# A second gather without a bound: an extra table row for edges whose source has no row of its own

## The reference

```python
x = _layernorm(x + _L0_gnn_ref(x, ...))          # mean of messages per node
# two relational attention layers, and a residual norm
h = x
for l in range(2):
    xw = einsum('nf,rfg->rng', h, W[l])
    out_j = xw[edge_type, src]; out_i = xw[edge_type, dst]
    logits = leaky_relu(out_i @ q[l] + out_j @ k[l])
    alpha = segment_softmax(logits, dst)
    h = relu(segment_sum(alpha * out_j, dst) + b[l])
x = _layernorm(x + h)
```

## Time and profile before

| | |
|---|---|
| median of 3 runs | 981.58 us (974.68 to 982.33) |
| the profiled execution | 986.6 us, span 984.5 us |
| TensorE's granted clock, mean | 0.835 of full speed |
| VectorE busy | 808.0 us (82%) |
| TensorE busy | 692.9 us (70%) |
| ScalarE busy | 613.8 us (62%) |
| GpSimd busy | 588.7 us (60%) |
| gathers of layer 0, first to last start | 325.4 to 481.5 us |
| gathers of layer 1, first to last start | 636.9 to 797.8 us |

### The profile page before, as it was taken

One profiled execution on the slowest core, in us unless ns is written; L12 is line 12 of the kernel. 1 busy time (PEld: TensorE's weight loads), 2 busy tenths in 40 slices (PEclk: granted clock), 3 DMA queues, 4 the chain that ended last, 5 costly groups with the idle time before them and its releaser, 6 DMA issues.

```text
span 984.5 us, 11352 instructions
## 1 busy us (share of the span) xinstructions
PE 692.9 (70%) x3092; PEld 444.9 (45%) x3092; DVE 808.0 (82%) x2191; ACT 613.8 (62%) x1396; POOL 588.7 (60%) x506
## 2 busy tenths in 40 slices
PE   3546657655664598898888889658899797678830
PEld 2425545444443365564554456434555453334410
DVE  4589997988889787889799999686878879999960
ACT  1569988997798755565557587554556463434440
POOL 4767777777770688888400000088887834876674
PEclk9657876787685599999999999769999897989975
DMA  8266666656554323225344554432222420143210
GB/s 222 83 207 192 200 194 203 200 171 198 174 158 133 99 79 99 84 69 183 114 133 125 162 163 135 140 103 87 68 67 96 157 69 28 48 136 90 64 39 28
DMA packets 87742, 123.00 MB, mean 125 GB/s; under 512 B 14174, under 2 KB 66826, under 8 KB 87679
## 3 DMA queue, kind: packets, MB, share of 16 engines
q1 hardware_dynamic: 69455, 99.35, 32.3%
q0 software_dynamic: 15680, 21.55, 7.8%
q10 hardware_dynamic: 2544, 1.38, 0.6%
HBM read 87.79 MB, written 45.04 MB: 135 GB/s over the span
## 4 chain that ended last, share of the span: by engine, by line
DVE 29%; POOL 23%; issue 18%; PE 10%; ACT 9%; DMA 8%; SPq 1%; POOLq 0%; DVEq 0%; ACTq 0%
POOL xs L461 19%; DVE ys L1121 5%; DVE work L1295 5%; POOL xd L461 4%; PE ps_y L714 4%; ACT stage L795 4%; DMA xs<-h_table,posI 3%; DVE st L1102 3%; DVE ys L1268 2%; DVE opT L1295 2%; DVE st L1071 2%; DMA xs<-x_table,posI 2%; ACT xd L811 2%; DVE st L1061 2%; DVE stage L1065 1%
## 5 line engine op out<-in xcount | busy, mean ns | idle before, releaser
L795 ACT ACTIVATE stage<-stage,nm,rs 128x128 f32<-128x128 f32 x800 | 320.8, 486 | 21.8 <-DVE nm L1056 21.8
L714 PE MATMUL ps_y<-work,wr 128*128 128x512 f32 (+1 forms) x528 | 232.7, 573 | 31.2 <-DVE work L1295 31.1
L461 POOL DMA_INDIRECT xs<-h_table,posI x98 | 132.7, 1354 | 183.9 <-DMA h_table<-ys 154.4
L461 POOL DMA_INDIRECT xs<-x_table,posI x98 | 127.6, 1302 | 62.2 <-DMA x_table<-xd 32.6
L1295 DVE SCALAR_TENSOR_TENSOR work<-typB,xs 128x896 f32<-128x896 uint8 x132 | 142.9, 1087 | 26.3 <-PE ps_y L714 18.9
L714 PEld LDWEIGHTS ps_y<-work,wr 128*128 128x128 f32 x528 | 100.7, 202 | 131.4 <-issue 73.5
L530 POOL DMA_INDIRECT out<-xd,outI x98 | 113.7, 1160 | 61.5 <-issue 28.7
L714 PE MATMUL ps_y<-opT,wr 128*128 128x512 f32 (+1 forms) x256 | 118.4, 588 | 23.7 <-DVE opT L1295 23.7
L461 POOL DMA_INDIRECT xs<-in_x,srcI x98 | 105.6, 1077 | 47.4 <-issue 28.4
L461 POOL DMA_INDIRECT xd<-in_x,dstG x98 | 107.3, 1095 | 29.9 <-issue 29.0
L1061 DVE BATCH_NORM_STATS2 st<-stage 128x6 f32<-128x128 f32 x400 | 82.9, 278 | 19.5 <-DMA stage<-in_x 19.1
(11 more groups left out here) (206 smaller groups left out, 1132.7 us busy)
## 6 DMA issues: line engine op xcount, KB each, us to landing
stage<-in_x SPq DMA_DIRECT2D x39, 640.0 KB, 4.1
out<-stage SPq DMA_DIRECT2D x39, 640.0 KB, 3.0
xs<-alpha_rows SPq DMA_DIRECT2D x28, 448.0 KB, 4.9
x_table<-xd SPq DMA_DIRECT2D x14, 448.0 KB, 3.0
h_table<-ys SPq DMA_DIRECT2D x14, 448.0 KB, 3.7
work<-in_src SPq DMA_DIRECT2D x13, 448.0 KB
ys<-in_edge_attr SPq DMA_DIRECT2D x6, 896.0 KB, 9.0
sameB<-same_rows SPq DMA_DIRECT2D x42, 112.0 KB
```

The lines of the kernel that those rows point to most:

```text
L461: nc.gpsimd.indirect_dma_start(out=buf[:, t, :], out_offset=None, in_=table, in_offset=bass.IndirectOffsetOnAxis(ap=idx[:, t:t + 1], axis= ...
L714: mm = pe.matmul(ps_y[:, u, lo:hi], wr[:, r, :], rows, start=(r == 0), stop=(r == R - 1))
L795: ins = a.activation(slot(c)[:, r, :], slot(c)[:, r, :], ACT.Identity, bias=nm[:, h, n:n + 1], scale=rs[:, h, n:n + 1])
```

## The change

`h1_table` gets row EP, and SP stores one partition of `relu_row` there once, late in stage A. VectorE makes a second list of indices for the second gather, min(pos, EP), in `dstG`, which stage A no longer needs. The layer-1 gather reads by `dstG` without a bound, so every row of `xs` is written. ScalarE's 14 fills, the semaphore `refill` and the order REFILLS are gone. The layer-0 gather is as it was.

```diff
-    REFILLS = [g for g in range(NG) if g != SPARE] + [SPARE]
...
-    h1_table = nc.dram_tensor("h1_table", (EP, D), F32).ap()
+    h1_table = nc.dram_tensor("h1_table", (EP + 1, D), F32).ap()
...
-        h1_rows = h1_table.rearrange("(t p) d -> p t d", p=P)
+        h1_rows = h1_table[0:EP].rearrange("(t p) d -> p t d", p=P)
...
                 if g == NG - 1:
+                    sp.dma_start(h1_table[EP:EP + 1, :], relu_row[0:1, 0, :]).then_inc(bare_out, 16)
                     sp.wait_ge(p_ready, 1)
                     sp.dma_start(wr[:], w_rel[0].rearrange("r f g -> f r g")).then_inc(w0_in, 16)
...
             for j in range(2):
-                pool.wait_ge(p_ready, 1)
+                pool.wait_ge(p_ready, j + 1)
                 for u in range(2):
                     pool.wait_ge(tab_out[j][u], 16 * NG // 2)
                 for g in range(NG):
-                    pool.wait_ge((a_norm, refill)[j], g + 1 if j == 0 else REFILLS.index(g) + 1)
-                    gather(g, xs, (x1_table, h1_table)[j], posI, xs_in[j + 1], EP - 1)
+                    if j == 0:
+                        pool.wait_ge(a_norm, g + 1)
+                        gather(g, xs, x1_table, posI, xs_in[1], EP - 1)
+                    else:
+                        if g == 0:
+                            pool.wait_ge(bare_out, 16)
+                        gather(g, xs, h1_table, dstG, xs_in[2])
...
-                def fill(g):
-                    copy(grp(xs, g), mid(relu_row[:, 0, :], G)).then_inc(refill, 1)
...
                             h1_out(s)
-                            if s not in (SPARE, NG - 1):
-                                fill(s)
...
-                if j == 0:
-                    fill(NG - 1)
-                    act.wait_ge(g_mul[0], NG)
-                    fill(SPARE)
...
                     T.step(v.tensor_copy(posI[:], lgC))
                     dve.sem_inc(p_ready, 1)
+                    T.step(TS(fmC, lgC, float(EP), None, ALU.min))
+                    T.step(v.tensor_copy(dstG[:], fmC))
+                    dve.sem_inc(p_ready, 1)
```

More of the change, by code:

```diff
@@ L264, in graph_layers @@
         g_T = [sem(f"g_T{j}") for j in range(2)]; last_used = sem("last_used")
-        refill = sem("refill")
+        bare_out = sem("bare_out")
         x_bulk = x[0:BC * BR * P].rearrange("(p r) d -> p r d", p=P)
```

## The result

| | median, us | of runs | ratio to before, 95% interval |
|---|---|---|---|
| before | 980.07 (974.68 to 982.33) | 4 | |
| after | 990.89 (985.51 to 997.38) | 4 | 1.0133 [1.0083, 1.0184] |

The change makes the kernel 1.3% slower by the ratio; the medians are 10.8 us apart. The forecast was 978.2 us, and the range ended at 986. The execution that was profiled took 997.38 us, its span is 995.5 us; the one of before had 984.5. Both are among the slower executions of their kernels, and the two traces differ by 11.0 us, about as the medians do.

The account below looks back on a forecast made before the run. The prediction took GpSimd's gather pace to bound the two gather stages and VectorE the second half of each layer. Bound -4.5, all rows moved +0.5 and two steps +0.6 gave -3.4 us, from 981.58 to 978.2 us; range 970 to 986.

Parts of the forecast that it names:

- All rows are moved now: Layer-1 gathers: moving 6.42 MB instead of 1.49 MB makes landings later, +0.5 us, bounds 0 and +1.5 us.
- one hot row: Rival, chance 0.05: layer-1 gathers read 77% of rows from one HBM address; at 27 GB/s, +18 us, some 997 us.
- the stage takes 181 us: Layer-1 gather stage under the hot-row rival: its length if one row gives 27 GB/s, +18 us.
- small delays of bulk loads: Layer-1 gather stage: delays from the higher DMA share, counted inside the +0.5 us for moving all rows.
- What would show it: Layer-1 stage signs: gather median near 0.947 us, stage 4 to 5 us shorter; wrong if landings pass 5 us.
- The bound goes: Layer-1 gathers: 0.053 us saved on each of 84 gathers, -4.5 us, bounds 0 and 27 us less.
- the bound is cheap, or the time is not passed on: Rival, chance 0.25: the 54 ns belong to table or stage, or VectorE delays gathers; +1.1 us, 982.7 us.
- Two more steps: VectorE, between posI and the last x1 rows' scales: two added steps on the path, +0.6 us, bounds 0.4 to 0.8.
- The fills: ScalarE: its 14 copies go; twelve are hidden, the last two precede a longer VectorE wait; 0 us.
- The sum: Whole kernel: -4.5 + 0.5 + 0.6 = -3.4 us, median 978.2 us; forecast given 0.50.
- The long gathers: Rival, chance 0.10: layer-1 gathers' mean falls to stage A's 1077 ns; -13 us, 968.5 us.
- The row by which the prediction explained the long gathers: Layer-1 gather at 655.78 us, 4.07 us long: held until VectorE's gapless run of two-SBUF-operand instructions ended.

Follow-up runs that it names:

- e1: The changed kernel with the extra row stored 128 times, partition p reading copy EP + p: 974.27 us (12 runs), 0.9976 of before.
- e7: The changed kernel with every index of the second gather set to the extra row, leaving out real source rows: 1051.93 us in one run.
- e8: The kernel before, each fill made by a DMA on ScalarE's queue reading the one row 896 times (448 KB): 1058.64 us in one run.
- e2: The changed kernel with the bound EP put back on the second gather, so no row is skipped: 995.87 us (4 runs), 1.0214 of before.
- e11: e1 with the bound EP + 127 on the second gather, which leaves out nothing: 978.46 us (12 runs), 1.0004 of before.
- e9: e1 with the two VectorE index steps moved some 3 us later, behind the flags hotE: 975.14 us (12 runs), 0.9941 of before.
- e10: The kernel of e5, two copies of the extra row, timed in twelve runs: 979.18 us, 0.9959 of before.
- e12: The kernel before with the two added VectorE steps alone, their result unused: 979.86 us (12 runs), 1.0016 of before.
- e3: The kernel before without ScalarE's 14 fills and the waits on them, leaving out nobody's-target rows: 977.05 us (10 runs), 1.0011 of before.
- e5: The changed kernel with copies of the extra row, partition p reading copy p mod 2: 965.91 us in one run, beside before at 979.54.

## Why the prediction was wrong, and where it was right

**The step that failed** is in "All rows are moved now": +0.5 us, with bounds of 0 and +1.5, "a later landing shifts the path once and not per group". Its bytes were right (6.4 MB), its price wasn't. It was taken from stage A, 3.7 us per MB, whose rows come from all over the input. e1 shows that this price holds for such rows (13.8%, share 0.39). With one address for 77% of them the same bytes took 60% of the engines' time. After and e1 differ in the address and the small steps that make it: 1.0133 against 0.9976 of before is 1.6%, some 15 us in time, and in the traces 199.4 against 175.7 us from the first gather to the scatter. So the term was some +15 us, not +0.5. The net loss in the trace, 13.3 us, has the gains of the other terms in it.

**The rival that came true** is *one hot row*, to which the prediction gave 0.05, at "some 997 us"; 990.9 was measured. That these are near each other is luck: 997 was worked out for a row of 27 GB/s against a need of 30, and by that reckoning a row with the 36 GB/s of e7 would have cost nothing. Two arguments had put it aside, and both were mis-sized:
- The demand was averaged, 30 GB/s over the 163 us. At the pace of the issue a gather starts every 1.25 us, and 0.77 x 64 KB / 1.25 us is 40 GB/s. e7 gives 36 to 37.5 GB/s for the row. So whenever GpSimd isn't held up, the queue grows: q0's share of the engines in the kernel after is 54.1% from 660 to 700 us, 75.2% to 740 and 85.8% to 780. With 1.83 MB in the last of these, 0.77 of it from the one row, the row gave 35 GB/s, the rate that e7 found for it.
- The `relu_row` load, 64 KB from one row in 2.9 us as a 0.5 KB load, was read as "cost no time that is visible". At 37 GB/s its 64 KB need 1.8 us, and this can lie inside the 2.9 us. A burst that short can't tell 37 GB/s from 100; the 448 KB of e8 can (16.5 us).

Also its mechanism was only half right: with it, "the stage takes 181 us", as though the gathers were paced by the row. They were not. Their stage got 16.5 us shorter, for GpSimd waited for a landing only 0.3 us in it, and in sum TensorE waited no longer for the rows than before (26.8 us, 29.9 before), though longer than in the seven kernels with a spread row (20.8 to 24.6 us). Most of the bill went to transfers that share the engines, the bulk loads and stores, and through them to VectorE. The text even named them ("small delays of bulk loads"), inside the 0.5 us. In "What would show it" two signs of error stood that both came: a landing above 5 us (6.2), and a gather stretch that gets shorter without the end moving (it moved the wrong way).

**The bound goes, -4.5 us.** The medians fell as said (1001 to 944 ns), and e2 and e11 show that it is the bound and not the table or the stage (997 and 999 ns with it). What it is in time is open: 3 to 6 us by the ratios of e11 against e1, e9 and e10, nothing by the medians of e11 and e10 and by the traces. Of the rival *the bound is cheap, or the time is not passed on* the first half is refuted, the second isn't.

**Two more steps, +0.6 us.** After, the CAST of `posI` is at 316.58 us and the scales' reciprocal at 317.54, 0.96 us apart, against 0.35 before: +0.61 us. In e9 it is 0.36 us again, and in e12 0.85, +0.50 us. From the CAST to the first layer-0 gather it is 7.7 us before and in e9, 8.3 after and 8.2 in e12, so the steps do delay that gather. In the times it can't be seen.

**The fills, 0 us.** e3: 1.0011 [0.9974, 1.0049]. ScalarE has 11.8 us less to do (602.0 for 613.8), and no time is seen to be won by it.

**The sum.** It was -3.4 us with the failed term at its forecast +0.5. The kernels in which the row is spread and the bound gone stand at -0.24% (e1), -0.41% (e10) and -0.59% (e9), -2.4 to -5.8 us; their medians lie 3.0, 0.3 and 4.4 us below those of before. That agrees with the sum in size. As the bound's share in it isn't shown, it doesn't confirm each term.

**The long gathers.** Their mean fell from 1354 to 1190 ns, where the rival that bears their name had 1077. The gathers of 4.07 us are still there. With the bound kept the mean is 1287 (e2) and 1285 (e11), so some 68 of the 164 ns aren't the bound's doing. Taken over the median, the mean excess is 353 ns before, 352 in e12, 301 in e1, 246 after and 219 in e7. The two lowest are the kernels in which VectorE stood still most, so GpSimd may have collided less because its neighbour was waiting, which is nothing won. This isn't shown: e2, with 28.9 us of waits for bulk loads, has 290 ns, and e11, with 17.1 us, has 286. The row by which the prediction explained the long gathers holds in part. The gather of 655.78 us began beside a mask that began at 655.50 and was held beyond it by two instructions that began after the gather, at 656.49 and 657.89 us.

## What to carry to other kernels

When many reads of a gather go to one default row, store that row several times and spread the readers over the copies; here two copies 512 bytes apart were enough to take the loss away, for one more column of numbers. It won at most 0.6% over the kernel with the fills. Compare the demand on a single address at the pace of the issue, not averaged over the stage, and measure the address with a load long enough to show a rate, since a burst disappears in the landing (64 KB and 0.5 KB both took 2.9 us). And where DMA engines are shared, look for the damage among the other queues' transfers: TensorE waited for the slow gathers no longer than before, and VectorE waited 27.7 us more for the loads beside them.

## What the runs showed of the hardware that was not expected

- One row of 512 bytes in HBM gave 36 to 37.5 GB/s to the 16 DMA engines together (e7), and 34 GB/s to ordinary DMAs (e8). Two neighbouring rows took the same demand with 15.7 to 16.3% of the engines' time where one took 64.5% (e5, e10 and after, 637 to 800 us). What in the memory sets this rate the runs don't show.
- Engines that wait for such a gather count as busy: share 1.00 at 99 GB/s after, 0.40 at 136 GB/s before, from 740 to 780 us. In e8 the same rate shows in the landings and much less in the shares: from 691 to 711 us the fills' queue moved 0.69 MB, 34.5 GB/s, at 22.5% of the engines' time, and a bulk store beside it landed after 19.7 us all the same. So a low DMA share doesn't clear a slow address; why the two forms are recorded so differently stays open.
- A bound costs an indirect gather of 128 rows of 512 bytes 53 ns (997 against 944 ns) even if it leaves out nothing (e2).
